# The one-head attention's weight products and first rows moved into the stage in front, and the mixture's small loads to the head of its queue

## The reference

```python
def _L3_attn_ref(x, Wq, bq, Wk, bk, Wv, bv, Wo, bo):
    q = jnp.einsum('bsd,ed->bse', x, Wq) + bq
    k = jnp.einsum('bsd,ed->bse', x, Wk) + bk
    v = jnp.einsum('bsd,ed->bse', x, Wv) + bv
    qk = jnp.einsum('bsd,btd->bst', q, k)
    theta = BASE_THETA + K_DOP * jax.nn.sigmoid(qk) + K_NOR * jnp.tanh(qk) + K_SERO * jax.nn.relu(qk)
    attn = jax.nn.softmax(theta, axis=-1)
    out = jnp.einsum('bst,btd->bsd', attn, v)
    return jnp.einsum('bsd,ed->bse', out, Wo) + bo
...
def _L3_ffn_ref(x, Wg, bg, W1, b1, W2, b2):
        gates = jax.nn.softmax(x @ Wg + bg, axis=-1)
        _, top_idx = jax.lax.top_k(gates, K)
        mask = jax.nn.one_hot(top_idx, E, dtype=gates.dtype).sum(axis=-2)
        g = gates * mask
        g = g / jnp.maximum(jnp.sum(jnp.abs(g), axis=-1, keepdims=True), EPS)
        h = jnp.einsum('btd,edh->bteh', x, W1) + b1[None, None]
        h = jax.nn.gelu(h, approximate=False)
        eo = jnp.einsum('bteh,ehd->bted', h, W2) + b2[None, None]
        return jnp.einsum('bte,btd->btd', g, eo)
```

## Time and profile before

| | us |
|---|---|
| runs | 1691.94, 1692.50, 1696.25; median 1692.50 |
| the profiled execution | 1691.59 |
| its span, first to last instruction | 1689.7 |
| `stage_xattn3`, 1352.61 to 1430.86 | 78.25 |
| `stage_attn3`, 1430.86 to 1478.35 | 47.49 |
| `stage_moe` up to its loop, 1478.35 to 1512.34 | 33.99 |
| the loop over 23 blocks and the end | 177.36 |

### The profile page before, as it was taken

How to read it: one execution, slowest core, us unless ns; L and a number is a source line. 1 busy time by engine, 2 the same in 40 slices (tenths; PEclk the granted TensorE clock), 3 DMA queues, 4 the chain that set the end, 5 groups by cost and what they waited for, 6 DMA issues and landing times. The chain is left out here.

```text
span 1689.7 us, 37134 instructions
## 1 busy us (share of the span) xinstructions
PE 1527.2 (90%) x13507; PEld 1317.3 (78%) x13507; DVE 1060.3 (63%) x2934; ACT 830.9 (49%) x2414; POOL 767.7 (45%) x894
## 2 busy tenths in 40 slices
PE   7999999988888999988999999997769697859998
PEld 6899999856567999976899999964459644649997
DVE  5888888556867788865877777749831142353332
ACT  5766666555336787852766666640014122113332
POOL 7665666353339999943211211228823311113332
PEclk9999999999999999998999999999969988969999
DMA  8655554212013333303533333343056272942221
GB/s 259 199 165 175 172 165 150 99 70 83 1 39 101 132 134 132 134 22 102 187 110 111 130 108 108 126 162 100 0 168 182 45 239 90 360 144 33 39 39 26
DMA packets 127222, 204.52 MB, mean 121 GB/s; under 512 B 21034, under 2 KB 92363, under 8 KB 126659
## 3 DMA queue, kind: packets, MB, share of 16 engines
q1 hardware_dynamic: 119016, 188.83, 34.3%
q0 software_dynamic: 6720, 8.79, 3.2%
q10 hardware_dynamic: 1306, 4.51, 0.8%
HBM read 161.76 MB, written 41.14 MB: 120 GB/s over the span
## 5 line engine op out<-in xcount | busy, mean ns | idle before, releaser
L1074 DVE TENSOR_SCALAR xattn_oT<-banks,xattn_last 128x256 f32<-128x256 f32 x254 | 111.1, 479 | 89.8 <-PE banks L854 89.2
L963 ACT ACTIVATE xattn_probs<-banks,xattn_negmax 128x257 f32<-128x257 f32 x256 | 123.3, 482 | 85.4 <-DVE xattn_negmax L1055 85.2
L968 ACT ACTIVATE xattn_probs<-xattn_probs,xattn_rsum 128x257 f32<-128x257 f32 x256 | 131.3, 513 | 1.4 <-DVE xattn_rsum L1059 1.4
L1351 POOL TENSOR_SCALAR xattn_probs<-xattn_probs,xattn_rsum 128x257 f32<-128x257 f32 x128 | 119.4, 933 | 23.9 <-DVE xattn_rsum L1624 23.1
L974 ACT CAST xattn_probsT_hi<-banks 128x256 fp32r<-128x256 f32 x256 | 94.8, 370 | 57.2 <-PE banks L829 57.2
L1055 DVE TENSOR_REDUCE xattn_negmax<-banks 128x1 f32<-128x257 f32 x256 | 106.2, 415 | 13.4 <-PE banks L820 12.0
L1064 DVE TENSOR_TENSOR xattn_probsT_lo<-banks,xattn_probsT_hi 128x256 fp32r<-128x256 f32 x256 | 105.5, 412 | 11.2 <-ACT xattn_probsT_hi L974 10.2
L765 POOL COPY ctx_stat<-xattn_mv 128x2 f32<-128x2 f32 x32 | 6.0, 187 | 225.0 <-DVE xattn_mv L1088 225.0
L829 PE MATMUL banks<-ident,xattn_probs 128*128 128x128 f32 x512 | 101.6, 281 | 6.2 <-ACT xattn_probs L968 5.7
L816 PE MATMUL banks<-xattn_ctxT,xattn_qk_hi 128*128 128x258 f32 x256 | 93.7, 366 | 0.5 <-DVE xattn_qk L1051 0.5
L715 POOL TENSOR_SCALAR xattn_ctxT<-xattn_rawT 128x514 fp32r<-128x514 f32 x32 | 49.9, 1558 | 88.7 <-issue 82.5
(11 more groups left out here) (516 smaller groups left out, 5093.8 us busy)
## 6 DMA issues: line engine op xcount, KB each, us to landing
xattn_ctxT<-ctx_partsT SPq DMA_DIRECT2D x64, 516.0 KB, 4.1
xattn_ctxN<-ctx_partsN SPq DMA_DIRECT2D x64, 384.0 KB, 4.1
ctx_partsT<-xattn_ctxT SPq DMA_DIRECT2D x32, 516.0 KB, 2.7
moe_w<-in_L_ffn_W SPq DMA_DIRECT2D x16, 1024.0 KB, 12.8
ctx_partsN<-xattn_ctxN SPq DMA_DIRECT2D x32, 384.0 KB, 3.5
moecap_w_early<-in_L_ffn_w SPq DMA_DIRECT2D x10, 1024.0 KB, 10.3
xattn_rawN<-in_ctx SPq DMA_DIRECT2D x32, 192.0 KB, 2.7
xattn_raw<-in_ctx SPq DMA_DIRECT2D x32, 192.0 KB, 5.2
```

The source lines that it names most:

```text
L963: nc.scalar.activation(probs[:, n % RING, :], SB[n % 2][:, 0:KV], ACT.Exp, bias=negmax[:, n % RING:n % RING + 1], accum_out=psum[:, n % RI ...
L968: nc.scalar.mul(probs[:, n % RING, :], probs[:, n % RING, :], rsum[:, n % RING:n % RING + 1]).then_inc(norm_ready, 1)
L1074: nc.vector.tensor_scalar(oT[k][:, heads, b, :], by_head(out_banks(n)[k][:, k * 2 * P:(k + 1) * 2 * P]), last[:, k, j * PER_TILE + b:j * P ...
L1351: nc.gpsimd.tensor_scalar(probs[:, n % RING, :], probs[:, n % RING, :], rsum[:, n % RING:n % RING + 1], None, ALU.mult).then_inc(norm_read ...
```

## The change

1. The weights of `attn3` move to a class `SoftWeights`. Its eight loads are issued by SP in `stage_moe_capacity`, behind the last expert's weights and ahead of the wait for the sums.
2. In `stage_xattn3`, POOL makes the two widened biases at the start. PE gets the folded biases at the end of step 8, `wq*wk` at the end of step 9, `wv*wo` at the end of step 10 and the transposes of tiles 0 to 3 at the end of step 11. ACT and DVE copy these out, and DVE takes the statistics of tiles 0 to 3 in step 9 and their rows in step 12.
3. `attn3` then goes the way of `attn1`: its first rows are there, tiles 4 to 7 are made inside it, and it makes tiles 0 to 3 of `stage_moe`. The values get a tile of their own, since `xn` is now needed. `stage_moe` makes only tiles 4 to 7, and the spare products of `Norm.warm` go in both stages.
4. The nine small inputs of `stage_moe` are issued ahead of the experts' weights, in `stage_attn3`, and `b1` and `b2` behind them, in the same list.

```diff
@@ stage_xattn3, pe
+                if s == FOLD_AT:
+                    pe.wait_ge(scaled_ready, TILES - 1)
+                    hw.fold_biases(pe, FOLD)
+                elif s == QUERIES_KEYS_AT:
+                    pe.wait_ge(scaled_ready, TILES)
+                    hw.queries_keys(pe, QUERIES_KEYS)
+                elif s == VALUES_OUT_AT:
+                    pe.wait_ge(probsT_ready, 2 * TILES)
+                    hw.values_out(pe, VALUES_OUT)
+                elif s == TURN_NEXT_AT:
+                    pe.wait_ge(o_ready, TILES)
+                    nx.turn(pe, 0, NEXT)
@@ stage_xattn3, vector
+                if s == FOLD_AT + 1:
+                    hw.take_biases(dve, FOLD)
+                    dve.wait_ge(x_done, 2)
+                    for t in Norm.HALVES[0]:
+                        nx.statistics(dve, t)
+                    nx.moments(dve, 0)
@@ stage_one_head, pe
-            if soft_theta:
-                ln.warm(pe, 7)
-                pe.wait_ge(loaded, 16 * LOADS)
-                product(QK, wq_s, wk_s).then_inc(qk_done, 1)
-                ln.pe(pe)
-                fold_biases()
-                product(VO, wv_s, wo_s).then_inc(vo_done, 1)
-                pe.wait_ge(qk_ready, 1)
+            pe.wait_ge(hw.qk_ready, 1)
             for n in range(2):
...
+                if n:
+                    ln.turn(pe, 1, LATE)
+                ln.transposed(pe, n)
@@ ExpertWeights
     def sp(self, sp):
+        self.gate.sp(sp)
+        sp.dma_start(self.token[:, :], d["token_number"]).then_inc(self.given_loaded, 16)
...
         self.rows.clear(sp)
         for e in range(self.E):
...
+        sp.dma_start(self.b1[:, :, :], d["L3_ffn_b1_cols"].rearrange("e p f -> p e f")).then_inc(self.loaded, 16)
+        sp.dma_start(self.b2[:, :, :], d["L3_ffn_b2"].partition_broadcast(P)).then_inc(self.loaded, 16)
@@ stage_moe, pe
-            ln.warm(pe, 7)
-            ln.pe(pe)
             for h in range(2):
-                pe.wait_ge(ln.xnT_ready, CD * (h + 1))
+                ln.transposed(pe, h)
                 gate.pe(pe, h)
+                if h == 0:
+                    ln.turn(pe, 1, LATE)
```

More of the change, by code:

```diff
@@ L2125, in _ @@
                 nc.gpsimd.tensor_tensor(x_plus[:, :, :], core.x[:, :, :], core.xn[:, :, :], ALU.add).then_inc(x_plus_ready, 1)
-                nx.power(pool, 0)
+            nx.power(pool, 0)
         @block.tensor
         def _(pe):
-            def product(out, left, right):
-                for c in range(CD):
-                    for k in range(CD):
-                        mm = nc.tensor.matmul(out[:, c * D:(c + 1) * D], left[:, k, c * P:(c + 1) * P], right[:, k, :],
-                                              start=(k == 0), stop=(k == CD - 1))
-                return mm
@@ L2232, in _ @@
                 values(t)
[L2233 to L2234 removed]
+            nx.take(act, 0, NEXT)
         @block.vector
         def _(dve):
[L2238 to L2243 removed]
+            for t in Norm.HALVES[1]:
+                ln.statistics(dve, t)
+            ln.moments(dve, 1)
             step = Chain(dve, steps)
             if soft_theta:
[L2246 to L2252 removed]
+                dve.wait_ge(hw.fold_ready, 4)
             for k in range(2 * CD):
                 n, f = divmod(k, CD)
[L2255 removed]
+                if k == 1:
                     ln.rows(dve, 1)
@@ L2298, in _ @@
                                                ALU.mult, ALU.add).then_inc(x_done, 1)
-                if t == 4 and not soft_theta:
+                if t == 4:
                     dve.wait_ge(x_done, 4)
@@ L2303, in _ @@
                     nx.moments(dve, 0)
-            if not soft_theta:
-                nx.rows(dve, 0)
+            nx.rows(dve, 0)
 def head_weights(core, ctx, outer):
@@ L3049, in sp, with stage_moe_capacity @@
             self.load(sp, e)
-def stage_moe_capacity(core, cw):
+def stage_moe_capacity(core, cw, hw):
     nc, d = core.nc, core.dram
@@ L3104, in _ @@
         def _(sp):
-            gate.sp(sp)
+            given.sp(sp)
             sp.dma_start(token[:, :], d["token_number"]).then_inc(loaded, 16)
@@ L3482, in _ @@
             pe.wait_ge(experts_ready, 1)
-            pe.wait_ge(ew.loaded, E * 32)
+            ew.ready(pe)
             turn_x(0)
@@ L3494, in _ @@
         def _(act):
-            ln.act(act)
+            ln.take(act, 1, LATE)
             gate.act(act)
@@ L3522, in _ @@
         def _(dve):
-            ln.dve(dve)
+            for t in Norm.HALVES[1]:
+                ln.statistics(dve, t)
+            ln.moments(dve, 1)
+            ln.rows(dve, 1)
             step = Chain(dve, steps)
@@ L3935, in _ @@
                         load_rows(act, s - 2 + RING)
+                if s == QUERIES_KEYS_AT + 1:
+                    hw.take_queries_keys(act, QUERIES_KEYS)
+                elif s == VALUES_OUT_AT + 1:
+                    hw.take_values_out(act, VALUES_OUT)
+            nx.take(act, 0, NEXT)
         @block.vector
@@ L3996, in _ @@
                     probs_turned(s - 1)
+                if s == TURN_NEXT_AT + 1:
+                    nx.rows(dve, 0)
                 if s >= 6 and s % 2 == 0:
```

283 lines of the change are left out of this document (147 added, 136 removed).

## The result

The median is 1694.68 us (1690.34 to 1707.46, 20 runs) against 1689.36 (1684.43 to 1696.25, 20 runs) for the kernel before on the same chip: a ratio of 1.0033, 95% interval [1.0018, 1.0047], so 5.3 us slower. On record stood 1693.8 against 1692.5, thus +1.3, with a range of 1686.0 to 1701.0. The kernel before is 3.1 us faster here than in the three runs that the forecast started from. One of the 10 executions of `b_first`, further down, took 5793.12 us; its ratio leaves it out, and without it the median is 1693.62.

What follows compares the result with a forecast made beforehand. PE's work in the unchanged mixture loop ends the chain of waits; the change acts on xattn3, attn3, ended by SP's list, and moe's head. +4.9 + 2.0 - 5.6 = +1.3 gave 1693.8 us against 1692.5, range 1686.0 to 1701.0.

Steps and rivals of the forecast that it cites:

- Term 1: Tail of xattn3: moved PE work of 7.8 us, partly hidden in PE's waits, lengthens the stage by 4.9 us.
- Term 2: attn3: compute shortens, but SP's issue list, with b1 and b2 stalling at its end, makes the stage 2.0 us longer.
- Term 3: Head of moe: with only tiles 4 to 7 made there, the logits are read earlier, saving 5.6 us.
- first rival: attn3: issues of b1 and b2 don't stall, costing 0.43 + 1.00; total -3.8 us, 1688.7; chance 0.20.
- second rival: attn3: SP doesn't hold the stage, which lasts 37.5 us; total -10.7 us, 1681.8; chance 0.10.
- third: attn3: both b1 and b2 stall, 11.6 us together, stage 54.6; total +6.4 us, 1698.9; chance 0.20.
- fourth: xattn3: moved products aren't covered by PE's waits, costing +11.3; total +7.7 us, 1700.2; sign xattn3 over 86; chance 0.05.

Runs made afterwards that it cites:

- b_first: The change with b1 and b2 issued in attn3 ahead of the sixteen expert weights instead of behind them; 1693.85 us, ratio 1.0008 to the kernel before.
- after_again: The change itself, unaltered, run once more for a second profile; 1695.82 us, ratio 1.0023 to the kernel before.
- split6: The change with the weights of experts 6 and 7, then b1 and b2, issued in stage_moe instead of attn3; 1678.82 us, ratio 0.9930.
- pb_split6: The change with folded biases and both weight products back in attn3, and experts 6 and 7's weights, b1 and b2 issued in stage_moe; 1676.42 us, ratio 0.9925.
- split6_act: split6 with the store of the rows' weights issued by ACT instead of SP; 1679.59 us, ratio 0.9944 to the kernel before.
- before_split6: The kernel before with only the weights of experts 6 and 7 issued in stage_moe, behind the stores of xn and x; 1693.38 us, ratio 1.0021.
- b_in_moe: The change with b1 and b2 issued in stage_moe, behind the store of the rows' weights, instead of ending attn3's list; 1687.32 us, ratio 0.9971.
- folds_back: The change with only the folded biases made in attn3 again, between the halves of t; 1693.58 us, ratio 1.0014 to the kernel before.

## Why the prediction was right, and where it was off

The time lies within the range and 0.9 from the forecast's 1693.8, and the mechanism held: SP's list sets the end of `attn3`, `xattn3` pays for the moved work, the head of `moe` gives most of it back. That the time comes so near is luck. The difference to the kernel before was forecast as +1.3 and is +5.3 (ratio 1.0033), four times as much; it is the lower median of the kernel before, 1689.36 for 1692.5, that hides it. Against this median the outcome lies just beyond the 5.1 us (0.3%) that the prediction calls no change, in the class "slower" that it gave 0.20. Step by step:

- **Term 1, +4.9.** It measured +6.0 to +6.2, in the last steps of `xattn3` (`after_again` and the first profile; +6.1 between the means of 7 and 5 profiles). The covers are as on record, three waits filled, 3.0, and the transposes cost nothing. Mis-sized are the folded biases, 4.0 to 4.35 for 3.1: the 3.1 was read at a clock of 1.00, and they ran at 0.80 in the change. The prediction had the clock only in its upper bound, whose factor of 1.45 comes from rows at 0.50 and 0.73. The first profile's +9.9 lies within that bound, but 3.7 of it is code that didn't change.
- **Term 2, +2.0.** It measured +4.3. The last weight's issue ended at 43.2 for 42.7 (put down as "between 0.5 later and 2.4 earlier"; it was 0.5 earlier), `b1` took 4.03 for 4.6. The step that failed is `b2` at 1.9, "nearer to the cheap one since `b1` itself is only 32 KB": it took 4.16. The two rows of the load behind six weights don't carry over: a stalled issue of 1024 rows of 32 bytes did not let the next one through cheaply. With 4.2 there, the list would have been put at 42.7 + 4.6 + 4.2 = 51.5 and the stage at 51.8, as measured; the two smaller errors cancel.
- The compute under it was put at 37.5 and is about 35 (split6). The last copy of t came at 11.3 as on record (11.5). The scores were taken unchanged from before and are not the same: from that copy to the next instruction of DVE it is 4.8 us, and 7.8 in the kernel before. In the change this was covered; in split6 it counts.
- **Term 3, -5.6.** It measured -4.9 (27.84 for 32.78, and 27.7 to 27.8 in eight other profiles); the reading of the logits stands at 10.6 for 9.9. Mis-sized is the copy of the last rows, 6.9 for 6.2, by the transposes at the lower clock.
- **The sum** of what was measured is 6.1 + 4.3 - 4.9 = +5.5, and the medians show +5.3. The +4.3 rests on one profile of either kernel, and between two profiles of the same code `attn3` differs by 0.9 (the change) and 2.4 (pb_split6), so part of this agreement is chance.
- The **first rival**, issues that don't stall, fell in the change itself, with 8.2 for its 1.4. That the place decides and not the shape is shown by b_first, 0.59 for 4.03. The Trainium skill (Perfetto Trace Analysis, Per-instruction lifecycle) puts the generation of descriptors into the profiled window; it also has a wait for the lock of the generator in it, which the prediction left out. In the change no other engine issued a DMA from 1401.8, in `xattn3`, to the end of `attn3`, and in split6_act ACT's issue of 0.39 passed inside a stalled one of SP, so no other engine's issue held SP up. What inside SP's own queue an issue waits for, no run here shows.
- The **second rival** fell in the change; in split6, with four weight issues moved out of the stage, its short stage came true, 35.1. The **third** had the right mechanism, both biases stalled, and too high a price, 11.6 for 8.2. The **fourth** fell, though the sign given for it, `xattn3` over 86, is there in the first profile with 88.17: PE's waits were filled all the same, and the second profile of the same code has 83.86.

What is open: why the granted clock of `xattn3` falls for longer in one execution than in another. The steps ahead of its last ones have the same instructions of PE in all fourteen profiles and took 56.2 to 62.4 us, a spread as large as what the moved work costs.

## What to carry over

Where all engines meet at a barrier, the queue that only issues transfers is an engine like the others: read where its list ends, and set that against the end of the compute, before work is moved out of the stage. Moving work away pays only up to that second bound: here 3.5 us, from the compute's end at 47.2 to the list's at 43.7, of the 12 that the compute got shorter. And an issue appended to a full queue costs what the queue needs, not what it cost elsewhere. Split the list over the next barrier as well: alone that won nothing (before_split6), the moved work alone lost 0.3%, and both together won 0.7%. Whether the two weight products and the folded biases are moved too or stay in `attn3` made no difference that could be told. And a product has no fixed duration: where the clock changes between executions, compare stages over several profiles, and cut them where the added work begins, so that the clock ahead of it drops out.

## What the runs showed of the hardware

- The same DMA of 1024 rows of 32 bytes took 0.43, 0.58, 0.59, 4.03 and 5.84 us to issue (before, b_in_moe, b_first, the change, split6_act), by what stood ahead of it on SP's queue.
- While SP stood in that issue of 5.84 us, ACT issued a DMA in 0.39. The transfer itself, 32 KB, still took 9.2 us to land behind the weights, and 2.1 where none stood ahead.
- With 16 MB on their way the DMA engines moved 376 GB/s with PE busy for 24.6 of 28.6 us (before) and 375 with PE idle (the change, 1470.0 to 1487.7). PE's clock was 1.00 from 1452.0 to 1468.8 and 0.50 from there on, while it was idle behind SP, and the first logits of the next stage ran at 0.50 (3.55 for the half).
- `wq*wk`, eight records of 128x256, took 1.99 us in the change, at a clock of 1.00, and 3.78 in folds_back, at 0.50, in the same step of `xattn3`.
